# Quantising the feed-forward weights in their own scale, on VectorE and ScalarE

## The reference

```python
def _quantize_elem(x, ebits, mfrac, max_norm):
    ax = jnp.abs(x)
    priv = jnp.floor(jnp.log2(jnp.where(ax == 0, 1.0, ax)))
    min_exp = float(-2 ** (ebits - 1) + 2)
    priv = jnp.maximum(priv, min_exp)
    scale = jnp.exp2(priv - mfrac)
    q = jnp.round(x / scale) * scale
    return jnp.clip(q, -max_norm, max_norm)

def _quantize_mx(x, ebits, mfrac, emax_elem, max_norm):
    xb = x.reshape(shp[:-1] + (shp[-1] // BLOCK, BLOCK))      # BLOCK = 32
    amax = jnp.max(jnp.abs(xb), axis=-1, keepdims=True)
    sexp = jnp.floor(jnp.log2(jnp.where(amax == 0, 1.0, amax))) - emax_elem
    scale = jnp.exp2(sexp)
    q = _quantize_elem(xb / scale, ebits, mfrac, max_norm) * scale

def _q_w(w): return _quantize_mx(w, 2, 1.0, 2.0, 6.0)
...
x = x + ffn(cond(x)); x = x + experts(gru(x))
```

## Time and profile before

| | us |
|---|---|
| median of 3 runs (1956.7 to 1957.79) | 1957.6 |
| span of the profiled execution, the slowest core | 1957.8 |
| the 24 pieces on VectorE (from its first reduction to its last clip) | 6.09 to 214.34 |
| setup until the first GRU step | to about 338 |
| VectorE busy over the span | 1636.9 (84%) |
| TensorE busy over the span | 1641.2 (84%) |
| GpSimd busy over the span | 643.7 (33%) |

### The profile page before, as it was taken

The page is one execution under the profiler, slowest core; times in us unless marked ns, Lnnn a source line. Parts: engine busy times, 40 slices in busy tenths (PEclk is TensorE's granted clock), DMA queues, the critical chain, the costliest instruction groups (busy, mean ns, idle before and its releaser), DMA issues. The chain is left out here.

```text
span 1957.8 us, 82261 instructions
## 1 busy us (share of the span) xinstructions
PE 1641.2 (84%) x32972; PEld 1251.9 (64%) x32972; DVE 1636.9 (84%) x5843; ACT 635.5 (32%) x1711; POOL 643.7 (33%) x795
## 2 busy tenths in 40 slices
PE   5422347999999999999999999999999999999976
PEld 2211115776777777777777777777777777777764
DVE  8999887888888888888888888888888888887653
ACT  1111223433333333333333333333333333333331
POOL 4545323333333333333333332333333333332111
PEclk8755568999999999999999999999999999999997
DMA  7313120000000000000000000000000000000100
GB/s 264 135 59 124 40 97 23 25 30 31 22 19 27 30 30 30 30 30 30 30 30 29 26 30 30 30 30 30 30 30 30 27 17 24 30 25 27 33 14 18
DMA packets 35405, 80.45 MB, mean 41 GB/s; under 512 B 4864, under 2 KB 5248, under 8 KB 34688
## 3 DMA queue, kind: packets, MB, share of 16 engines
q1 hardware_dynamic: 28080, 63.09, 9.6%
q10 hardware_dynamic: 6992, 12.13, 1.8%
HBM read 58.43 MB, written 16.78 MB: 38 GB/s over the span
## 5 line engine op out<-in xcount | busy, mean ns | idle before, releaser
L1294 PE MATMUL ps_rn<-hx,whh 128*128 128x32 f16 x16384 | 451.2, 176 | 85.0 <-DVE hx L715 47.4
L1294 PEld LDWEIGHTS ps_rn<-hx,whh 128*128 128x128 f16 x16384 | 430.9, 96 | 129.8 <-DVE hx L715 90.3
L1016 POOL COPY hT_steps<-hx 128x128 f16<-128x128 f16 x256 | 120.2, 469 | 992.3 <-DVE hx L715 992.3
L1187 PE MATMUL ps_gi<-x1T,wih 128*128 128x128 f16 x4608 | 289.6, 219 | 1.2 <-ACT gi L523 1.2
L1187 PEld LDWEIGHTS ps_gi<-x1T,wih 128*128 128x128 f16 x4608 | 271.3, 98 | 25.9 <-issue 1.7
L532 ACT ACTIVATE r<-r_pre,scale 128x64 f32<-128x64 f32 x256 | 89.0, 348 | 581.6 <-DVE r_pre L735 581.6
L1294 PE MATMUL ps_z<-hx,whh 128*128 128x32 f16 x8192 | 244.2, 176 | 0.0
L1294 PEld LDWEIGHTS ps_z<-hx,whh 128*128 128x128 f16 x8192 | 223.5, 96 | 0.1
L523 ACT ACTIVATE gi<-ps_gi,b_i,scale_x 128x128 f32 (+1 forms) x384 | 144.4, 456 | 159.1 <-PE ps_gi L1187 159.1
L1003 POOL TENSOR_TENSOR qf<-f8c,fe 128x512 bf16<-128x512 bf16 x128 | 135.8, 1061 | 148.4 <-DVE f8c L796 148.4
L1120 PE MATMUL ps_gate_up<-wq,qxT 128*128 128x512 bf16 x512 | 143.6, 397 | 19.5 <-issue 15.0
(11 more groups left out here) (198 smaller groups left out, 2885.2 us busy)
## 6 DMA issues: line engine op xcount, KB each, us to landing
wih<-in_x_steps ACTq DMA_DIRECT2D x32, 256.0 KB, 5.5
xin<-in_x_steps SPq DMA_DIRECT2D x32, 256.0 KB, 4.0
xres<-in_x_steps SPq DMA_DIRECT2D x32, 256.0 KB, 4.1
x_dram<-x SPq DMA_DIRECT2D x32, 256.0 KB, 2.9
x_in<-x_dram SPq DMA_DIRECT2D x32, 256.0 KB, 2.7
out_rows<-y SPq DMA_DIRECT2D x32, 256.0 KB, 2.0
wst<-in_ffn_w SPq DMA_DIRECT2D x12, 512.0 KB, 3.4
sg_gs<-in_ffn_w SPq DMA_DIRECT2D x12, 512.0 KB, 3.7
```

What stands on the lines that cost most here:

```text
L1016: g.tensor_copy(hT_steps[:, :, s, :], hx[:, :, :, :].rearrange("p k u b -> p (k u) b"))\
L1187: last = mm(ps_gi[:, j * P:(j + 1) * P], wih_parts[:, k, at:at + P], x1T[:, x, k, :], start=k + w + x == 0, stop=k == KD - 1 and w == 1)
L1294: last = mm(ps[:, (at + j) * 2 * B:(at + j + 1) * 2 * B], whh[:, k, u, gate * D + j * P:gate * D + (j + 1) * P], hx[:, k, :, :].rearrange( ...
```

## The change

All numbers of a piece are now formed in the piece's own scale, so that no scaled copy is made and GpSimd has no part in a piece.

- SyncE loads the pieces into three buffers in `gi` (`AHEAD`); the load of piece p waits for the eighth count of VectorE's work on piece p - 3, that of L585.
- ScalarE, `upper_half`, copies the upper 16 bits of each weight (a bf16 view with a step of two) into `wyh`, and writes them turned within each chunk of 128 features: from 4 blocks of 32 to 32 rows of 4. It does so two pieces ahead of its copy out of PSUM.
- VectorE works on 16-bit numbers: L570 keeps the exponent bits, L573 takes the largest of each block (a reduction with a step of 4 elements, 8 bytes), L576 makes rounding constants of the exponents, L577 those of the blocks, L579 takes the larger of both into `wm` (the blocks' operand is read again for each k), L580 and L581 form the upper and lower limits; L585 adds `wm` to the float32 weights, which it reads turned (32 elements, 128 bytes, from one to the next, four times, then back), L587 subtracts it, L589 and L592 clip. All in order, each waiting for the one before where it reads its result.
- The features within a chunk of 128 are in turned order in `wq`; therefore GpSimd writes `qf` and `qx` turned in the main loop too (L1010, L1053; output step 4 elements).
- The block sums take three x tiles in each of the first 11 pieces instead of four in each of 8, and the middle pieces are no longer a loop but written out.

```diff
-SUM_PARTS = 8
+SUM_PARTS = 11
+SUM_TILES = 3
...
+EXP_MASK_HIGH = 0x7F80
...
+AHEAD = 3
...
+def by_blocks(ap):
+    return ap.rearrange("p (c k n) -> p c k n", k=MXB, n=P // MXB)
+def by_chunk_of_features(ap):
+    return ap.rearrange("p (c n) -> p c n", n=P // MXB)
+def over_blocks(ap):
+    by_chunk = by_chunk_of_features(ap)
+    return by_chunk.unsqueeze(2).broadcast_to([P, by_chunk.shape[1], MXB, P // MXB])
...
-        wst = [sb("wst0", [P, PIECE]), sg_gs[:, 0:PIECE]]
+        wst = [gi[:, u * PIECE:(u + 1) * PIECE] for u in range(AHEAD)]
+        wyh = [x[:, :].bitcast(BF16) for x in (x1_in, x1_bias, y)]
+        bt_flat = bt[:, :, :].rearrange("p m n -> p (m n)").bitcast(BF16)
+        wm, wqk, wt = bt_flat[:, 0:PIECE], bt_flat[:, PIECE:2 * PIECE], sg_gs[:, 0:PIECE]
         qfT_flat = qfT[:, :, :].rearrange("p k n -> p (k n)")
-        wy = [gi[:, u * PIECE:(u + 1) * PIECE] for u in range(2)]
-        wm = [gi[:, 2 * PIECE:3 * PIECE], sb("wm1", [P, PIECE])[:, :]]
         wqn = [qfT_flat[:, u * PIECE:(u + 1) * PIECE] for u in range(2)]
-        wam, we, wnew, wsc, winv = ([sb(f"{x}{u}", [P, PIECE // MXB]) for u in range(2)]
-                                    for x in ("wam", "we", "wnew", "wsc", "winv"))
+        wam, wsc, wtop, wlow = (sb(x, [P, PIECE // MXB], BF16) for x in ("wam", "wsc", "wtop", "wlow"))
...
-            def piece(turn, u):
-                wait(sp, w_y, count_piece(turn, u, -1))
-                wait_apart(sp, passed)
-                at = (turn * 2 + u) * P
-                src = ffn_w[at:at + P, :] if isinstance(turn, int) else ffn_w[bass.ds(at, P), :]
-                sp.dma_start(wst[u][:, :], src).then_inc(w_loaded[u], 16)
+            def piece(p):
+                wait(sp, w_m, (p - AHEAD) * 10 + 8)
+                sp.dma_start(wst[p % AHEAD], ffn_w[p * P:(p + 1) * P, :]).then_inc(w_loaded[p % AHEAD], 16)
...
-                first = (p + 1) * TILES // SUM_PARTS if p else 0
-                for t in range(first, min((p + 2) * TILES // SUM_PARTS, TILES)):
+                first = (p + 1) * SUM_TILES if p else 0
+                for t in range(first, min((p + 2) * SUM_TILES, TILES)):
...
-            def piece(turn, u):
-                ps = (ps_up, ps_z)[u]
-                act.wait_ge(w_mm, count_piece(turn, u, 1))
-                nc.scalar.activation(wq[:, bass.ds(turn * 2 + u, 1), :], ps[:, :].bitcast(BF16).unsqueeze(1),
-                                     ACT.Copy).then_inc(w_ev, 1)
+            def upper_half(p):
+
+                act.wait_ge(w_loaded[p % AHEAD], (p // AHEAD + 1) * 16)
+                wait(act, w_m, (p - AHEAD) * 10 + 5)
+                upper = wst[p % AHEAD].bitcast(BF16)[:, 1::2].rearrange("p (c n k) -> p c n k", n=P // MXB, k=MXB)
+                nc.scalar.activation(by_blocks(wyh[p % AHEAD]).rearrange("p c k n -> p c n k"), upper,
+                                     ACT.Copy).then_inc(w_yh, 1)
+
+            def piece(p):
+                if p == 0:
+                    upper_half(0)
+                    upper_half(1)
+                if p + 2 < PIECES:
+                    upper_half(p + 2)
+                ps = (ps_up, ps_z)[p % 2]
+                act.wait_ge(w_mm, p + 1)
+                nc.scalar.activation(wq[:, p:p + 1, :], ps[:, :].bitcast(BF16).unsqueeze(1), ACT.Copy).then_inc(w_ev, 1)
...
-            def scales(turn, u):
-                k = count_piece(turn, u) * 4
-                dve.wait_ge(w_loaded[u], (turn + 1) * 16)
-                v.tensor_reduce(wam[u][:, :], blocked(wst[u][:, :]), AX_X, ALU.max,
-                                apply_absolute_value=True).then_inc(w_small, 1)
-                dve.wait_ge(w_small, k + 1)
-                v.tensor_scalar(we[u][:, :].bitcast(U32), wam[u][:, :].bitcast(U32), EXP_MASK, None,
-                                ALU.bitwise_and).then_inc(w_small, 1)
-                dve.wait_ge(w_small, k + 2)
-                wait(dve, w_kept_sc, count_piece(turn, u, -1))
-                v.tensor_scalar(wnew[u][:, :], we[u][:, :], TINY, 0.25, ALU.max, ALU.mult).then_inc(w_small, 1)
-                dve.wait_ge(w_small, k + 3)
-                v.reciprocal(winv[u][:, :], wnew[u][:, :]).then_inc(w_small, 1)
-            def piece(turn, u):
-                if not (isinstance(turn, int) and turn == TURNS - 1 and u == 1):
-                    scales(turn + u, 1 - u)
-                k = count_piece(turn, u) * 3
-                wait(dve, w_out, count_piece(turn, u, -1))
-                v.tensor_copy(wsc[u][:, :], wnew[u][:, :]).then_inc(w_kept_sc, 1)
-                dve.wait_ge(w_y, count_piece(turn, u, 1))
-                v.tensor_scalar(wm[u].bitcast(U32), wy[u].bitcast(U32), EXP_MASK, None,
+            def piece(p):
+                u, at = p % AHEAD, p * 10
+                dve.wait_ge(w_yh, p + 1)
+                v.tensor_scalar(wyh[u].bitcast(U16), wyh[u].bitcast(U16), EXP_MASK_HIGH, None,
                                 ALU.bitwise_and).then_inc(w_m, 1)
-                dve.wait_ge(w_m, k + 1)
-                v.tensor_scalar(wm[u], wm[u], 1.0, ROUND_STEP, ALU.max, ALU.mult).then_inc(w_m, 1)
-                dve.wait_ge(w_m, k + 2)
-                v.scalar_tensor_tensor(wy[u], wy[u], -6.0, wm[u], ALU.max, ALU.add).then_inc(w_m, 1)
-                dve.wait_ge(w_m, k + 3)
-                v.scalar_tensor_tensor(wy[u], wy[u], 4 * ROUND_STEP + 6.0, wm[u], ALU.min, ALU.subtract)\
-                    .then_inc(w_q, 1)
+                dve.wait_ge(w_m, at + 1)
+                v.tensor_reduce(by_chunk_of_features(wam[:, :]), by_blocks(wyh[u]).rearrange("p c k n -> p c n k"), AX_X,
+                                ALU.max).then_inc(w_m, 1)
+                dve.wait_ge(w_m, at + 2)
+                v.tensor_scalar(wyh[u], wyh[u], ROUND_STEP, None, ALU.mult).then_inc(w_m, 1)
+                v.tensor_scalar(wsc[:, :], wam[:, :], TINY, 0.25 * ROUND_STEP, ALU.max, ALU.mult).then_inc(w_m, 1)
+                dve.wait_ge(w_m, at + 4)
+                v.tensor_tensor(by_blocks(wm), by_blocks(wyh[u]), over_blocks(wsc[:, :]), ALU.max).then_inc(w_m, 1)
+                v.tensor_scalar(wtop[:, :], wsc[:, :], 6.0 / ROUND_STEP, None, ALU.mult).then_inc(w_m, 1)
+                v.tensor_scalar(wlow[:, :], wsc[:, :], -6.0 / ROUND_STEP, None, ALU.mult).then_inc(w_m, 1)
+                dve.wait_ge(w_m, at + 5)
+                by_weights = wst[u].rearrange("p (c n k) -> p c k n", n=P // MXB, k=MXB)
+                v.tensor_tensor(by_blocks(wt), by_weights, by_blocks(wm), ALU.add).then_inc(w_m, 1)
+                dve.wait_ge(w_m, at + 8)
+                v.tensor_tensor(wqk, wt, wm, ALU.subtract).then_inc(w_m, 1)
+                dve.wait_ge(w_m, at + 9)
+                v.tensor_tensor(by_blocks(wqk), by_blocks(wqk), over_blocks(wtop[:, :]), ALU.min).then_inc(w_m, 1)
+                dve.wait_ge(w_m, at + 10)
+                wait(dve, w_mm, p - 1)
+                v.tensor_tensor(by_blocks(wqn[p % 2]), by_blocks(wqk), over_blocks(wlow[:, :]),
+                                ALU.max).then_inc(w_out, 1)
...
-            def scale_piece(turn, u):
-                wait(pool, w_out, count_piece(turn, u, -1))
-                pool.wait_ge(w_small, count_piece(turn, u, 1) * 4)
-                g.tensor_tensor(blocked(wy[u]), blocked(wst[u][:, :]), spread(winv[u][:, :]),
-                                ALU.mult).then_inc(w_y, 1)
-            def piece(turn, u):
-                if not (isinstance(turn, int) and turn == TURNS - 1 and u == 1):
-                    scale_piece(turn + u, 1 - u)
-                pool.wait_ge(w_q, count_piece(turn, u, 1))
-                wait(pool, w_mm, count_piece(turn, u, -1))
-                g.tensor_tensor(blocked(wqn[u]), blocked(wy[u]), spread(wsc[u][:, :]), ALU.mult).then_inc(w_out, 1)
+            def turned_blocks(t):
+                return by_blocks(t[:, :]).rearrange("p c k n -> p c n k")
+            def chunks_of_blocks(t):
+                return t[:, :].rearrange("p (c n k) -> p c n k", n=P // MXB, k=MXB)
+            def spread_chunks(t):
+                return by_chunk_of_features(t[:, :]).unsqueeze(3).broadcast_to([P, KD, P // MXB, MXB])
...
-                        g.tensor_tensor(blocked(qf[:, :]), blocked(f8c[:, :]), spread(fe16[:, :]),
+                        g.tensor_tensor(turned_blocks(qf), chunks_of_blocks(f8c), spread_chunks(fe16),
...
-                    g.tensor_tensor(blocked(qx[:, :]), blocked(q8c[:, :]), spread(qe16[:, :]),
+                    g.tensor_tensor(turned_blocks(qx), chunks_of_blocks(q8c), spread_chunks(qe16),
...
-            scale_piece(0, 0)
-            over_pieces(pool, piece, nothing, attention, slot)
+            over_pieces(nothing, nothing, attention, slot)
```

46 lines of the change are left out of this document (20 added, 26 removed).

## The result

The changed kernel takes 2021.96 us (median of 4 runs, 2014.24 to 2025.45) where the kernel before takes 1957.69 beside it: a ratio of 1.0309, 95% interval 1.0279 to 1.0339. It is 3.1% slower, where 0.8% faster was forecast. Its profiled execution took 2023.99 us, its span is 2022.2.

The account below looks back on a forecast made before the run. TensorE bounds the main loop, left alone; VectorE, held up by GpSimd, was the one to watch in the setup. 1957.8 - 17.3 + 1.3 = 1941.8 us of span, so 1941.6 us; range 1926 to 1966 for 8 in 10.

Parts of the forecast that it names:

- The main loop: Loop over the tiles: TensorE's work left alone, GpSimd's `qf` unchanged in time, loop as long as before.
- `qf`: GpSimd's product in the main loop, written with a step of 8 bytes: 1.05 us, bounds 1.05 to 1.26.
- the rule drawn from L977 and L986: GpSimd's time does not follow bytes written: 1.91 us with 4-byte output as with 2-byte output.
- The rule for the price: Fourth step of a tile: each 0.1 us more on `qf` costs 0.1 us per tile; at 1.26, 6 us.
- The piece: One weight piece on VectorE in the setup: 7.37 us instead of 8.09, over 24 pieces 17.3 us gained.
- L585: VectorE's sum in a piece, weights read 128 bytes apart: 1.23 plus 0.56 us, 1.79 us.
- my row: L612, 128 floats read 64 bytes apart in 0.346 us, used to price L585's step at 0.55 ns per element.
- the turned read: Rival in VectorE's pieces: L585 and L573 dearer, 1.12 us more per piece, 1968 us; decides from 0.67 us; 15%.
- the 16-bit mode: Rival in VectorE's pieces: two-tensor 16-bit operations go element by element, a piece of 9.02 us, 1981 us; 6%.
- The start: Setup start: VectorE waits for a load and one upper half, beginning at 7.35 instead of 6.09; 1.3 us lost once.
- The rest of the setup: VectorE's other work between the pieces: stays at 14.1 us, with 4 us either way.
- What is covered: ScalarE's work per piece, 3.7 us of 7.4, and the loads stay hidden; lost cover would cost some 2 us once.

Follow-up runs that it names:

- after_straight: The changed kernel with GpSimd's `qf` and `qx` written in straight order, mixing wrong features: 2022.90 us, ratio 1.0320.
- 182 increments: Changed kernel with 182 semaphore increments nobody waits for on TensorE ahead of the tile loop: 1945.62 us; with straight `qf` and `qx` 1942.64 us.
- 227: Changed kernel with 227 semaphore increments nobody waits for on TensorE ahead of the tile loop: 1986.98 us; with straight `qf` and `qx` 1971.54 us.

## Why the prediction was wrong

**The step that failed is "The main loop".** It took the loop as unchanged but for `qf`, since no instruction in it changed. What changed was where the loop lies in TensorE's stream, 29 machine instructions later, and that was worth +71 us in the loop, four times the whole forecast gain; the same 29 without the change cost the kernel before 70.7 us. The trace of before had the rows for it: a pause of 1.2 to 1.7 us at every loop top, and one after 98 matmuls, together 15.0 us in 22 passes (the row below: busy time and mean ns, then idle time and what ended it); and the diff puts 16 transposes more ahead of the loop. I read neither. No rival had this mechanism, and the time lies outside the range of 1926 to 1966.

```profile
L1120 PE MATMUL ps_gate_up<-wq,qxT 128*128 128x512 bf16 x512 | 143.6, 397 | 19.5 <-issue 15.0
```

**`qf`** was taken at 1.05 us, with 1.26 as the upper bound. It is 1.34 us; the rule drawn from L977 and L986, that GpSimd's time doesn't follow what it writes, does not hold for a step between the elements (and 1.91 was the shortest of L977's twelve; their median was 2.25). The rule for the price, 0.1 us per tile for each 0.1 us, was near in size: 0.29 x 29 would be 8 us; 5.4 were measured, half of it in the fourth step as foreseen and half at the tile's end. Beside the pauses it was anything from nothing (`after_straight`) and 3 us (182 increments) to 15 (227) and 17 (kernel before), by their place.

**The piece** was 7.37 us by the forecast and is 7.59, so it gains 0.50 us and not 0.72. Right to 0.03 us: the reduction with its step (1.22), both single-source operations (0.42, 0.43), the three 16-bit operations on two tensors (0.69), and L587. The term that was mis-sized is L585, at 1.79:

```profile
L585 DVE TENSOR_TENSOR sg_gs<-gi,bt x24: 1896/1920/1974, 11.6 to 200.8; 128x1024 f32<-128x1024 f32 x24
```

That is 1.92 in the median, 0.69 more than 1.23, or 0.67 ns per element where the row gave 0.55; 24 x 0.13 = 3 us, and the rest of the 24 x 0.22 = 5.3 us is small change, 0.01 to 0.04 us in most of the gaps. By the 1.73 ns that section 5.2 of "Vector Engine (DVE) Microarchitecture Reference" of the Trainium skill gives for one source that hops 4 KiB at every element it would be, by estimate, 1.92, and the trace has that at 128 bytes; my row, 128 floats of one partition, was low. The rivals on VectorE fell: the turned read is dearer by 0.13 us and not by the 0.67 from which its rival decides, and the 16-bit mode is not slow.

**The start** cost 2.5 us and not 1.3, because ScalarE's write with a step of 8 bytes takes 2.48 us; I had priced it by a copy that writes straight, and looked only at its source.

**The rest of the setup** came out near the forecast, but by luck. 14.1 us of other work on VectorE were left, and (205.37 - 8.62) - 24 x 7.59 = 14.6 are there. 4.0 of them are a wait for ScalarE that "What is covered" had at nothing: the upper half of the nineteenth piece stands behind a copy (`proj`) that waits for TensorE, in the order of ScalarE's instructions, and ScalarE's share of busy time did not show that.

```profile
151.44 0.60 ACT L466 ACTIVATE proj<-ps_base 128x512 f32<-128x512 f32 x1 [5.75 <-PE ps_base L1109]
151.93 2.47 ACT L434 ACTIVATE x_in<-gi 128x1024 bf16<-128x1024 bf16 x1
154.44 0.43 DVE L570 TENSOR_SCALAR x_in<-x_in 128x1024 uint16<-128x1024 uint16 x1 [3.96 <-ACT x_in L434]
```

It is made up for by operations that GpSimd's products of the pieces no longer hold up: four of them (L588, L593, L616 and L779 of before) took 7.7 us and take 1.3, the one into `xn` 2.40 and now 0.68. The setup was forecast to end 17.3 - 1.3 = 16.0 us earlier, and L692 comes 8.9 earlier: 5.3 for the piece, 1.3 for the start and 0.5 for the rest are the 7.1 between.

Where the loop does not branch, the whole change is worth 2.8 us instead of 16.
